# Graph network on one core: three buffers of counts in place of four in the first pass, the fourth's room given to one-hots that are made further ahead, and 53 dense tiles in place of 54

## The chip, the core and the metric

One core of a Trainium2 chip (trn2) runs the whole program. The metric is the device time of one execution in microseconds; it is compared by the median of several runs. The clock of the multiply engine, TensorE (PE in the rows), is granted at one of two levels, 1.2 or 2.4 GHz; a row shows it as a share of the full one.

## What is computed

12500 nodes with 64 features, 212500 directed edges sorted by destination, two layers:

```python
x = x + layer0(relu(layernorm(x)), edge_attr, src, dst)
x = x + layer1(relu(layernorm(x)), src, dst)

def layer0(h, e, src, dst):
    agg = segment_sum(h[src] + e, dst)
    h = relu(agg @ W1 + b1) @ W2 + b2
    return batch_norm(h)

def conv(h, W, b):                       # layer1: conv, relu, conv, relu, then a norm over the graph
    return segment_sum((h @ W)[src] * enorm[:, None], dst) + b
```

So there are three sums over the edges, one for each of three passes, and before each a table of node features is ready in memory.

## The kernel before

**Two ways to sum over edges.** For the first D windows of 125 destination nodes (D = 54 in the first pass, 69 in the other two) the sum is *dense*: a tile of counts A, 12500 sources by 125 destinations in fp8, is multiplied with the table that lies in SBUF (`app`, 100 matmuls for a tile in 25 steps of 4). All other edges are *gathered*: groups of 1280 edges, whose table rows POOL fetches by ten indirect DMAs into one of four slots (`pool_pass`), are summed on PE through a matrix S of destinations (`grp`). The edges' own features, in the first pass alone, are summed in groups too: 167 groups in all, each with an S, a split of the features into three bf16 parts on DVE (`rest1`, `rest2`) and ten matmuls; the groups with a gather have ten more. How many groups have a gather follows from D: `QG` is 88 for 54 tiles, so 79 groups of the first pass are gathered.

**The counts are built on the chip.** A tile of counts comes from 32 products on PE (`bld`) of two one-hots that DVE makes: `oh` (L954, one for a product) and `ob` (L951, one for four products). Each two products fill one of two PSUM banks (`NBANK = 2`), which ACT moves to the tile in SBUF (`evict`, L1204); a product of a new pair waits for the one-hot and for the eviction of the pair two before it:

```python
pe.wait_ge(v_oh, v + 1)
pair, s = v // 2, v % 2
if s == 0 and pair >= NBANK:
    pe.wait_ge(a_ev, pair - NBANK + 1)
```

A finished tile is used by 100 matmuls, and stored to memory (`keep`, 1.6 MB) for the later passes, which load it (`fetch`). The first pass builds all its 54 tiles, the second builds 17 and loads 52, the third loads all 69. Four slots (`NA = 4`) hold tiles of counts. A one-hot lies in one of 6 buffers (`NOH`), an `ob` in one of 3 (`NOB`); DVE waits with a new one until the product that read the buffer is done.

**The order of the work** is written by `make_plan`: every step of an engine gets a due time in units, where one unit is one step of 4 `app` matmuls, and each engine runs its steps in the order of these times, one after another. In the first pass tile q is built from unit 25q, 32 products in 25 units; it is applied from unit 31 + 25q. A group stands every 8 units or so: at t its matmuls, at t + 2.4 the fold of its PSUM on DVE (`fold_q`, L987), at t + 4.6 a transpose on PE (`turn`, L1185; L1189 for a tile's window), 2.1 units later DVE's addition to the accumulator (`add`, L1015, L1020). The next transpose waits for that addition. When all windows of four node blocks are done, a small perceptron runs (`hid`, L1137; `up`, L1140; `hout`, `hmean`, `hvar` on ACT). Due times are no waits: what holds an engine are its semaphores, and the steps queued behind a waiting one.

## Time and profile before

| | |
|---|---|
| median of 3 runs | 4469.84 us (4464.91 to 4476.29) |
| the profiled execution, own time | 4486.21 us |
| its span | 4484.9 us (1.3 us less than its own time) |
| mean granted TensorE clock | 0.809 |
| first pass, first to last fold of a tile (L997) | 219.1 to 1879.9 us |
| busy share of the span | PE 67%, DVE 43%, POOL 42%, ACT 18% |

A busy PE is not PE at its peak, since matmuls overlap: their durations are longer than their distance. The chain of work in the profile names the engine whose work ended last at each step; "remote" and "another core or an unknown queue" stand where the record of a semaphore's rise is missing.

### The profile page before, as it was taken

What the parts mean: (1) busy time and instruction counts of PE and PEld (TensorE: products, weight loads), DVE (VectorE), ACT (ScalarE), POOL (GpSimd) and SP (SyncE); (2) the same over time, 40 slices, a digit from 0 to 9 for tenths busy, and PEclk for the clock granted to TensorE, in tenths of its full rate; (3) what the DMA queues carried; (4) which work ended last, traced back from release to release, by engine and by line L of the source; (5) the groups of instructions that cost most, each with busy time, mean ns of one, the idle gap of its engine ahead of it and who ended that gap; (6) DMA issues with size and microseconds to landing.
All of it is one profiled execution on the core that took longest, in us unless ns stands there. A gap on an engine that the chain in (4) does not pass through costs nothing.

```text
span 4484.9 us, 66591 instructions
## 1 busy us (share of the span) xinstructions
PE 3012.4 (67%) x26545; PEld 2766.3 (62%) x26545; DVE 1926.5 (43%) x4856; ACT 796.3 (18%) x1708; POOL 1861.6 (42%) x1895
## 2 busy tenths in 40 slices
PE   1366676676666667737777777777847777776777
PEld 1365565566556556636666676666846666666667
DVE  9476676767667667742333332323301111111112
ACT  6122222222222223332111111111100000000000
POOL 4554444545444442032444433444134444444441
PEclk9988788878877788858778878888968778878878
DMA  5243333434334333443333333333443333333334
GB/s 125 78 115 100 96 111 99 118 96 116 99 94 114 96 111 101 118 124 119 113 99 114 127 99 127 100 116 126 140 120 113 126 111 127 113 111 119 119 126 123
DMA packets 359879, 504.29 MB, mean 112 GB/s; under 512 B 302486, under 2 KB 302679, under 8 KB 334736
## 3 DMA queue, kind: packets, MB, share of 16 engines
q1 hardware_dynamic: 298437, 402.60, 27.6%
q0 software_dynamic: 60512, 94.12, 9.3%
q8 instruction: 219, 3.59, 0.3%
q10 hardware_dynamic: 616, 3.20, 0.3%
q14 instruction: 95, 0.78, 0.1%
HBM read 362.65 MB, written 137.13 MB: 111 GB/s over the span
## 4 chain that ended last, share of the span: by engine, by line
PE 50%; another core or an unknown queue 17%; issue 14%; DVE 13%; ACT 3%; DVEq 1%; DMA 1%; SPq 0%; POOL 0%; ACTq 0%; POOLq 0%
PE psum L1102 34%; PE psum L1084 6%; DVE arena L954 4%; PE psum L1124 3%; PE psum L1117 3%; DVE arena L980 2%; DVE arena L951 2%; ACT arena L1204 1%; DVEq L1013 1%; PE psum L1067 1%; DVE arena L964 1%; PE psum L1189 1%; PE psum L1137 1%; PE psum L1185 1%
## 5 line engine op out<-in xcount | busy, mean ns | idle before, releaser
L1265 POOL DMA_INDIRECT arena<-table,srcT x1840 | 1800.2, 978 | 2300.3 <-PE psum L1124 1638.2
L1102 PE MATMUL psum<-arena 125*125 125x193 bf16 (+1 forms) x19200 | 2374.5, 274 | 404.9 <-issue 356.6
L1102 PEld LDWEIGHTS psum<-arena 125*125 125x125 fp8e4 x19200 | 2108.8, 157 | 499.6 <-issue 460.6
L1084 PE MATMUL psum<-arena 128*125 128x200 f16 x2272 | 609.0, 287 | 594.4 <-issue 263.0
L954 DVE TENSOR_SCALAR arena<-iota,keyT,oddT 128x200 f16<-128x200 f16 x2272 | 700.8, 336 | 613.2 <-remote 374.4
L1204 ACT CAST arena<-psum 125x400 uint16<-125x400 f32 x1136 | 549.4, 492 | 2148.3 <-PE psum L1084 1236.2
L1084 PEld LDWEIGHTS psum<-arena 128*125 128x125 f16 x2272 | 344.5, 157 | 686.5 <-DVE arena L954 359.4
L951 DVE TENSOR_TENSOR arena<-modT,psum 128x500 f16<-128x500 f16 x568 | 376.4, 663 | 0.1
L964 DVE SCALAR_TENSOR_TENSOR arena<-relT,psum 128x960 bf16<-128x960 f16 x272 | 310.8, 1143 | 0.0
L997 DVE TENSOR_REDUCE arena<-psum 125x64 f32<-125x192 f32 x192 | 67.2, 350 | 562.5 <-PE psum L1102 288.8
L980 DVE TENSOR_TENSOR arena<-arena 128x650 f32<-128x650 f32 (+1 forms) x334 | 274.4, 822 | 7.0 <-DMA arena<-in_edge_attr_dram 4.8
L1117 PE MATMUL psum<-arena 128*96 128x195 bf16 (+1 forms) x1662 | 215.0, 285 | 2.3 <-DVE arena L980 2.3
L1247 ACT ACTIVATE cneg<-cst 125x1 f32<-125x1 f32 x25 | 5.1, 203 | 1189.8 <-DVE arena L1039 1039.0
L987 DVE TENSOR_REDUCE arena<-psum 96x65 f32<-96x195 f32 (+1 forms) x275 | 96.5, 351 | 273.2 <-PE psum L1124 270.9
L1124 PE MATMUL psum<-arena 128*96 128x192 bf16 x1846 | 198.6, 258 | 3.9 <-DMA arena<-table,srcT 3.9
L1117 PEld LDWEIGHTS psum<-arena 128*96 128x96 bf16 (+1 forms) x1662 | 191.1, 145 | 2.8 <-issue 2.5
L1189 PE MATMUL psum<-ident,arena 125*64 125x125 f32 x192 | 60.5, 315 | 190.3 <-DVE arena L997 117.6
L1124 PEld LDWEIGHTS psum<-arena 128*96 128x96 bf16 x1846 | 177.3, 132 | 4.4 <-DMA arena<-table,srcT 4.2
L996 DVE COPY cnt<-psum 125x1 f32<-125x1 f32 x123 | 19.4, 158 | 371.9 <-remote 217.5
L1020 DVE SCALAR_TENSOR_TENSOR acc<-psum,acc 64x125 f32<-64x125 f32 x192 | 53.3, 277 | 270.0 <-remote 192.4
L1015 DVE SCALAR_TENSOR_TENSOR acc<-psum,acc 65x96 f32 (+1 forms) x275 | 68.6, 249 | 205.3 <-PE psum L1185 146.2
L1189 PEld LDWEIGHTS psum<-ident,arena 125*64 125x64 f32 x192 | 23.5, 122 | 215.2 <-issue 188.5
(207 smaller groups left out, 1000.2 us busy)
## 6 DMA issues: line engine op xcount, KB each, us to landing
arena<-counts SPq DMA_DIRECT2D x121, 1600.0 KB
counts<-arena SPq DMA_DIRECT2D x71, 1600.0 KB
arena<-in_edge_attr_dram SPq DMA_DIRECT2D x166, 320.0 KB
arena<-table,srcT POOLq DMA_INDIRECT x1840
table<-arena SPq DMA_DIRECT2D x8, 1050.0 KB
table<-arena SPq DMA_DIRECT2D x25, 168.0 KB
arena<-table SPq DMA_DIRECT2D x4, 1050.0 KB
arena<-in_x_dram ACTq DMA_DIRECT2D x4, 700.0 KB
```

Source lines behind the costliest of these rows:

```text
L951: dve.tensor_tensor(ob(four % NOB), mod, it, ALU.is_equal)
L954: dve.tensor_scalar(oh(v % NOH), iota1[:, :], keyT[:, v:v + 1], oddT[:, v:v + 1], ALU.is_equal, ALU.mult).then_inc(v_oh, 1)
L964: dve.scalar_tensor_tensor(out=S, in0=rel, scalar=0.0, in1=it, op0=ALU.add, op1=ALU.is_equal).then_inc(v_S, 1)
L980: dve.tensor_tensor(ebuf(e, i + 1)[0:parts, 0:nt * FE], a, upper, ALU.subtract).then_inc(v_rest1 if i == 0 else v_rest2, 1)
L987: dve.tensor_reduce(qbuf(n % 2)[:, 0:fe], ps_q.rearrange("p (s f) -> p f s", s=3)[:, 0:fe, :], X, ALU.add).then_inc(v_fq, 1)
L1084: pe.matmul(to, ob(v // NB4 % NOB)[:, v % NB4, :], oh(v % NOH).rearrange("p (j m) -> p j m", m=2), start=True, stop=True).then_inc(p_bld, 1)
L1102: last = pe.matmul(ps_v[n % 2][0:PN, 0:xc], A(slot)[0:PN, j, 0:PN], Xs[0:PN, j, 0:xc], start=(j == 0), stop=(j == J - 1))
L1117: last = pe.matmul(ps_q, S[0:parts, t, :], e3(v % NEDGE)[0:parts, t, :, :], start=(t == 0), stop=(t == nt - 1 and not gathered))
L1124: last = pe.matmul(to, S[0:parts, t, :], gbuf(slot)[0:parts, t, :].rearrange("p (s f) -> p s f", s=3), start=(k > 0 and t == 0), stop=(t = ...
L1189: pe.transpose(ps_g[0:F, 0:PN], vbuf(m % 2)[0:PN, :], ident[0:PN, 0:PN]).then_inc(p_win, 1)
L1204: act.copy(A2(slot)[0:PN, :, i // 2 * SUB:(i // 2 + 1) * SUB], ps_b[b // 2 % NBANK][0:PN, :].rearrange("p (j x) -> p j x", x=SUB)).then_in ...
L1265: pool.indirect_dma_start(out=gbuf(slot)[0:parts, t, :], out_offset=None, in_=tables[k], in_offset=bass.IndirectOffsetOnAxis(ap=idx, axis= ...
```

## The change

In the first pass alone, tiles of counts use three slots (`NA0 = 3`) and not four. The room of the fourth holds 14 more `oh` and 4 more `ob`, so that 20 and 7 are there in place of 6 and 3. DVE makes a product's one-hot 14 units ahead of it, where it was 3.3 (14 units are 18 products, 3.3 units are 4). S, `rest1` and `rest2` of a group are put 3 units earlier, the load of its edges 2 units earlier. `hmean` and `hvar` are put about a unit later. The first pass has 53 dense tiles, which the three slots ask for (`D0 % NA0 == 2`), so `QG` is 87 and 80 groups are gathered; the second pass builds 18 tiles, one in three from the seventh on, and loads 51. The x load at the end of the first pass goes where slots 2 and 3 are, so it waits for all products too.

```diff
-NOH = 6
+NOH = (20, 6)
-NOB = 3
+NOB = (7, 3)
 NA = 4
+NA0 = 3
-DENSE = (54, 69, 69)
+DENSE = (53, 69, 69)
...
-            if n_b < len(built) and q >= 6 and (q - 5) * len(built) >= n_b * (D - 7):
+            if n_b < len(built) and q >= 6 + 3 * n_b:
...
-                dve.append((t - 3.3, "oh", b))
+                dve.append((t - (14.0 if k == 0 else 3.3), "oh", b))
...
-        dve.append((t - 7.0, "S", n))
+        dve.append((t - (10.0 if k == 0 else 7.0), "S", n))
         if k == 0:
-            sp.append((t - 12.5, "edges", n))
-            dve.append((t - 5.2, "rest1", n))
-            dve.append((t - 4.2, "rest2", n))
+            sp.append((t - 14.5, "edges", n))
+            dve.append((t - 8.2, "rest1", n))
+            dve.append((t - 7.2, "rest2", n))
...
-            act.append((t + 6.2, "hmean", i))
-            act.append((t + 6.4, "hvar", i))
+            act.append((t + 7.3, "hmean", i))
+            act.append((t + 7.4, "hvar", i))
...
+        def slot_of(k, q):
+            return q % NA0 if k == 0 else (plans[k]["s0"] + q) % NA
...
-                    if v >= NOH:
-                        dve.wait_ge(p_bld, v - NOH + 1)
+                    if v >= noh:
+                        dve.wait_ge(p_bld, v - noh + 1)
...
-                        if q >= NA:
-                            act.wait_ge(p_app, n - NA + 1)
+                        if q >= (NA0 if k == 0 else NA):
+                            act.wait_ge(p_app, n - (NA0 if k == 0 else NA) + 1)
...
                 sp.wait_ge(p_app, D0 - 2)
-                for i in (2, 3):
-                    sp.wait_ge(st_cnt[i], kept[0][i])
+                sp.wait_ge(p_bld, NB0)
+                sp.wait_ge(st_cnt[2], kept[0][2])
```

What this does to DVE's order shows at two places. The first is DVE at the start of the first pass (L951 and L954 are `ob` and `oh` of before, L964 is S, L980 a `rest`); before:

```order
L951 TENSOR_TENSOR arena<-modT,psum 128x500
L954 TENSOR_SCALAR arena<-iota,keyT,oddT 128x200 x4
L951 TENSOR_TENSOR arena<-modT,psum 128x500
L954 TENSOR_SCALAR arena<-iota,keyT,oddT 128x200 x3
L964 SCALAR_TENSOR_TENSOR arena<-relT,psum 128x960
```

and of the changed kernel, where the same steps have the lines L965, L968 and L978:

```order
L965 TENSOR_TENSOR arena<-modT,psum 128x500
L968 TENSOR_SCALAR arena<-iota,keyT,oddT 128x200 x4
L965 TENSOR_TENSOR arena<-modT,psum 128x500
L968 TENSOR_SCALAR arena<-iota,keyT,oddT 128x200 x4
L965 TENSOR_TENSOR arena<-modT,psum 128x500
L968 TENSOR_SCALAR arena<-iota,keyT,oddT 128x200 x4
L965 TENSOR_TENSOR arena<-modT,psum 128x500
L968 TENSOR_SCALAR arena<-iota,keyT,oddT 128x200 x4
L965 TENSOR_TENSOR arena<-modT,psum 128x500
L968 TENSOR_SCALAR arena<-iota,keyT,oddT 128x200
L978 SCALAR_TENSOR_TENSOR arena<-relT,psum 128x960
```

Ahead of the first S there stand 17 one-hots of products where there were 7.

The second place is DVE in the middle of the first pass, from one group's `add` on (L1015; L987 is `fold_q`); before:

```order
L1015 SCALAR_TENSOR_TENSOR acc<-psum,acc 65x96
L954 TENSOR_SCALAR arena<-iota,keyT,oddT 128x200
L951 TENSOR_TENSOR arena<-modT,psum 128x500
L954 TENSOR_SCALAR arena<-iota,keyT,oddT 128x200 x2
L964 SCALAR_TENSOR_TENSOR arena<-relT,psum 128x960
L954 TENSOR_SCALAR arena<-iota,keyT,oddT 128x200 x2
L987 TENSOR_REDUCE arena<-psum 96x65
L951 TENSOR_TENSOR arena<-modT,psum 128x500
L954 TENSOR_SCALAR arena<-iota,keyT,oddT 128x200
L980 TENSOR_TENSOR arena<-arena 128x650
L954 TENSOR_SCALAR arena<-iota,keyT,oddT 128x200
L980 TENSOR_TENSOR arena<-arena 128x650
```

and of the changed kernel (L1029 is the `add`, L994 a `rest`, L1001 the `fold_q`, L978 S):

```order
L1029 SCALAR_TENSOR_TENSOR acc<-psum,acc 65x96
L968 TENSOR_SCALAR arena<-iota,keyT,oddT 128x200 x2
L994 TENSOR_TENSOR arena<-arena 128x650
L968 TENSOR_SCALAR arena<-iota,keyT,oddT 128x200
L994 TENSOR_TENSOR arena<-arena 128x650
L965 TENSOR_TENSOR arena<-modT,psum 128x500
L968 TENSOR_SCALAR arena<-iota,keyT,oddT 128x200 x2
L1001 TENSOR_REDUCE arena<-psum 96x65
L968 TENSOR_SCALAR arena<-iota,keyT,oddT 128x200 x2
L965 TENSOR_TENSOR arena<-modT,psum 128x500
L968 TENSOR_SCALAR arena<-iota,keyT,oddT 128x200 x3
L978 SCALAR_TENSOR_TENSOR arena<-relT,psum 128x960
```

Before, S stands ahead of the fold and the two `rest` behind it; in the changed kernel the two `rest` stand ahead of the fold and S behind it.

## Rows read from the trace of the kernel before

**Rows 1.** The page: span, busy time of each engine, granted clock by slice.

```profile
span 4484.9 us, 66591 instructions
PE 3012.4 (67%) x26545; PEld 2766.3 (62%) x26545; DVE 1926.5 (43%) x4856; ACT 796.3 (18%) x1708; POOL 1861.6 (42%) x1895
```

**Rows 2.** Windows: window, length, busy of five engines (count), clock, DMA.

```profile
200.00:1740.00 1540.00, 1026.24 (x8633) 926.87 (x8630) 1076.19 (x2739) 403.86 (x867) 739.11 (x720) 0.81 0.38 104
1740.00:1880.00 140.00, 114.58 (x1064) 101.62 (x1064) 122.15 (x316) 49.11 (x108) 2.25 (x2) 0.92 0.44 131
2050.00:3200.00 1150.00, 839.89 (x7515) 783.30 (x7513) 367.65 (x1073) 156.68 (x335) 466.27 (x492) 0.81 0.35 112
```

**Rows 3.** One line, L997 (a tile's fold), 200 to 1740, then 1740 to 1885.

```profile
L997 DVE TENSOR_REDUCE arena<-psum x47: 337/344/358, 219.1 to 1719.2; 125x64 f32<-125x192 f32 x47
L997 DVE TENSOR_REDUCE arena<-psum x7: 339/344/347, 1752.9 to 1879.9; 125x64 f32<-125x192 f32 x7
```

**Rows 4.** Windows of 4 us over one burst of gathers.

```profile
840.00:844.00 4.00, 2.60 (x28) 2.27 (x27) 4.00 (x12) 1.15 (x3) 3.09 (x4) 1.00 0.46 102
844.00:848.00 4.00, 2.23 (x24) 1.88 (x21) 0.46 (x3) 0.49 (x1) 3.09 (x4) 1.00 0.20 44
848.00:852.00 4.00, 0.00 (x0) 0.00 (x0) 1.33 (x2) 0.00 (x0) 2.34 (x3) 0.88 0.21 42
852.00:856.00 4.00, 2.34 (x15) 2.37 (x16) 2.97 (x7) 1.38 (x3) 0.00 (x0) 0.50 0.36 82
```

**Rows 5.** Timeline, 846 to 854: start, length, engine, what, [idle before it].

```profile
846.42 0.36 PE L1084 MATMUL psum<-arena 128*125 128x200 f16 x2 [0.89 <-issue]
...
853.02 0.89 ACT L1204 CAST arena<-psum 125x400 uint16<-125x400 f32 x2 [6.75 <-remote]
853.03 0.33 DVE L954 TENSOR_SCALAR arena<-iota,keyT,oddT 128x200 f16<-128x200 f16 x1 [3.69 <-remote]
...
853.63 0.18 PEld L1084 LDWEIGHTS psum<-arena 128*125 128x125 f16 x1 [6.70 <-DVE arena L954]
853.66 0.40 PE L1084 MATMUL psum<-arena 128*125 128x200 f16 x1 [6.54 <-ACT arena L1204]
```

**Rows 6.** Waits, 200 to 1850: total us, times, longest.

```profile
PEld psum L1084 <- DVE arena L954: 291.9, 146, 8.0
DVE arena L954 <- remote: 259.8, 112, 6.7
...
PE psum L1084 <- ACT arena L1204: 199.6, 78, 7.8
...
DVE arena L954 <- PE psum L1084: 171.2, 175, 3.2
...
PEld psum L1137 <- DVE acc L1015: 24.5, 17, 3.6
PEld psum L1189 <- DVE acc L1015: 22.2, 16, 2.6
...
PEld psum L1185 <- DVE acc L1020: 13.9, 13, 3.0
...
DVE arena L980 <- DMA arena<-in_edge_attr_dram: 2.4, 2, 1.4
```

**Rows 7.** Timeline: first and last product that waited for a one-hot.

```profile
241.07 0.35 PEld L1084 LDWEIGHTS psum<-arena 128*125 128x125 f16 x2 [0.76 <-DVE arena L954]
...
1837.88 0.13 PEld L1084 LDWEIGHTS psum<-arena 128*125 128x125 f16 x1 [0.54 <-DVE arena L954]
```

**Rows 8.** Lines by form, 200 to 1850: gathers on POOL.

```profile
L1265 POOL DMA_INDIRECT arena<-table,srcT x720 | 739.3, 1027 | 802.5 <-PE psum L1124 601.8 <-issue 197.5 <-remote 3.1
```

**Rows 9.** Timeline, 1346 to 1355: a store of counts, then loads of edges.

```profile
1346.06 0.33 SPq L1303 DMA_DIRECT2D counts<-arena  x1
...
1346.43 5.74 SPq L1299 DMA_DIRECT2D arena<-in_edge_attr_dram  x2
...
1354.27 0.84 DVE L980 TENSOR_TENSOR arena<-arena 128x650 f32<-128x650 f32 x1 [1.04 <-DMA arena<-in_edge_attr_dram]
```

More of the change, by code:

```diff
@@ L210, in bass_gnn_preln_kernel @@
     SHIFT = RED * NSUB
-    assert NSUB % NB4 == 0 and NB4 * PN % 2 == 0 and 2 * KC <= 512 and NROW * P <= E and NC * P <= 5 * 512 and D0 % NA == 2 and NSUB % 2 == 0
+    assert NSUB % NB4 == 0 and NB4 * PN % 2 == 0 and 2 * KC <= 512 and NROW * P <= E and NC * P <= 5 * 512 and D0 % NA0 == 2 and NSUB % 2 == 0
     assert NBLD - SEED <= 2048 and SUB == 4 and P % NSUB == 0
@@ L234, in bass_gnn_preln_kernel @@
         n_oh = KC // 2
-        o_ob = o_oh + NOH * n_oh
+        o_ob = o_oh + NOH[1] * n_oh
         n_ob = NB4 * PN // 2
-        o_hb = o_ob + NOB * n_ob
+        o_hb = o_ob + NOB[1] * n_ob
+        o_ox = o_A + NA0 * n_A
+        n_ox = (NOH[0] - NOH[1]) * n_oh + (NOB[0] - NOB[1]) * n_ob
+        assert n_ox < (NA - NA0) * n_A
         o_g = max(o_hb + 2 * JH * PN, o_e + JF)
@@ L329, in oh @@
         def oh(k):
-            return part(o_oh, k, n_oh).bitcast(F16)
+            at = part(o_oh, k, n_oh) if k < NOH[1] else part(o_ox, k - NOH[1], n_oh)
+            return at.bitcast(F16)
         def ob(k):
-            return part(o_ob, k, n_ob).bitcast(F16).rearrange("p (n d) -> p n d", d=PN)
+            o = o_ox + (NOH[0] - NOH[1]) * n_oh
+            at = part(o_ob, k, n_ob) if k < NOB[1] else part(o, k - NOB[1], n_ob)
+            return at.bitcast(F16).rearrange("p (n d) -> p n d", d=PN)
         def ebuf(k, i=0):
@@ L526, in sp_load @@
                              a.rearrange("(a b) -> a b", a=1).broadcast_to([P, 1])).then_inc(l_w, 16)
-            n = NA * n_A
-            spare = x.rearrange("p n -> (p n)")[0:(P - PN) * n].rearrange("(a n) -> a n", n=n)
-            sp.dma_start(arena[PN:P, o_A:o_A + n], spare).then_inc(l_spare, 16)
+            for a, b in ((o_A, o_ox), (o_ox + n_ox, o_w)):
+                spare = x.rearrange("p n -> (p n)")[0:(P - PN) * (b - a)].rearrange("(a n) -> a n", n=b - a)
+                sp.dma_start(arena[PN:P, a:b], spare).then_inc(l_spare, 16)
         LN_ORDER = (3, 2, 0, 1)
@@ L901, in bass_gnn_preln_kernel @@
             for q, (kind, w) in enumerate(pl["seq"]):
-                slot = (pl["s0"] + q) % NA
+                slot = slot_of(k, q)
                 kept_before[k, q] = n_kept[slot]
@@ L1083, in pe_pass @@
                     to = ps_b[pair % NBANK][0:PN, :].rearrange("p (j s m) -> p j s m", s=2, m=2)[:, :, s, :]
-                    pe.matmul(to, ob(v // NB4 % NOB)[:, v % NB4, :], oh(v % NOH).rearrange("p (j m) -> p j m", m=2), start=True,
+                    pe.matmul(to, ob(v // NB4 % NOB[k])[:, v % NB4, :],
+                              oh(v % NOH[k]).rearrange("p (j m) -> p j m", m=2), start=True,
                               stop=True).then_inc(p_bld, 1)
@@ L1088, in pe_pass @@
                     n = pl["d0"] + q
-                    slot = (pl["s0"] + q) % NA
+                    slot = slot_of(k, q)
                     if i == 0:
@@ L1196, in act_pass @@
                     n = pl["d0"] + q
-                    slot = (pl["s0"] + q) % NA
+                    slot = slot_of(k, q)
                     if i == 1:
-                        if q >= NA:
-                            act.wait_ge(p_app, n - NA + 1)
+                        if q >= (NA0 if k == 0 else NA):
+                            act.wait_ge(p_app, n - (NA0 if k == 0 else NA) + 1)
                         if kept_before[k, q]:
@@ L1284, in sp_fetch @@
             pl = plans[k]
-            slot = (pl["s0"] + v) % NA
+            slot = slot_of(k, v)
             if kept_before[k, v]:
@@ L1300, in sp_pass @@
                 elif kind == "keep":
-                    slot = (pl["s0"] + v) % NA
+                    slot = slot_of(k, v)
                     sp.wait_ge(a_ev, last_b[k, v])
@@ L1799, in sp_first @@
             sp.wait_ge(v_set, 1)
-            sp.wait_ge(l_spare, 16)
+            sp.wait_ge(l_spare, 2 * 16)
         def pe_second():
```

11 lines of the change are left out of this document (7 added, 4 removed).

## The prediction

> **What bounds the kernel now.** The page comes first: the span is 4484.9 us and no engine fills it, PE comes nearest with 67% [rows 1]. So the limit is in how the engines wait for each other, and it has to be read by stage. The windows cut the run into stretches [rows 2]. In the first pass, while gathers run (200 to 1740), PE is busy 67% and DVE 70% (1076 of 1540 us). In its last 140 us, when the gathers are over, PE is busy 82% and DVE 87%. In the second pass DVE has 32%. The folds of the tiles give the pace [rows 3]: with gathers (1719.2 - 219.1) / 46 = 32.6 us for a tile, without them (1879.9 - 1752.9) / 6 = 21.2 us. The gathers are what makes a tile long, though POOL itself often waits for PE, 601.8 us of 1650 [rows 8].
>
> Windows of 4 us over one burst of ten gathers show how [rows 4]. At its start DVE is full (4.00 of 4.00). From 844 on PE fades, from 848 to 852 it does nothing and DVE a third. Then it starts again at clock 0.50. The timeline says what ends this [rows 5]: the two products that PE issued at 846.42 are seen by ACT and by DVE only at 853.02 and 853.03, when the burst is over, and PE goes on at 853.63. So semaphores that PE raises during a burst reach the others late, by up to some 6 us, and PE stops when it meets a wait whose answer depends on one of them.
>
> **Which wait that is** decides what this change can do. The waits view names both [rows 6]: the load of a product's weights (PEld) is put down to DVE's one-hot with 291.9 us, the multiplication (PE) to ACT's eviction with 199.6 us. It is the same idle time under two names, as in rows 5 (6.70 and 6.54 us). To part them I took each of the 1654 products between 200 and 1850 and compared the start of its load with the end of its own one-hot and of the eviction that it needs. 219 products stand behind more than 0.3 us of idle, 475.6 us in all. In 194 of them, 461.3 us, the eviction ended last; in 25, 14.4 us, the one-hot did; the first and the last of these 25 stand in [rows 7]. PE is stopped by the two PSUM banks, and the change leaves them at two.
>
> **The change part by part.**
>
> *The moved tile.* The first pass loses 100 `app` matmuls and 32 products. Without gathers 140 us hold 1064 matmuls, 0.132 us each [rows 2]: -17.4 us. By the stretch with gathers (1540 / 8633 = 0.178 us) it would be -23.5; I take the first, since a burst's stop belongs to the burst.
>
> *One more gathered group.* Bursts per tile: 72 groups (720 gathers) in 1540 / 32.6 = 47.2 tiles, 1.53 [rows 2, 3, 8]. One costs (32.6 - 21.2) / 1.53 = 7.5 us. Lower bound: the idle of one stop, some 5 us; upper: a burst's whole length, 10 x (1.03 + 0.30) = 13.3 us [rows 8]. I take +7.5.
>
> *32 products more in the second pass*, at 1150 / 7515 = 0.153 us a matmul [rows 2]: +4.9 us. A store takes the place of a load; DMA engines are at 0.35 there, so that costs nothing. The new spacing of the built tiles only shifts work.
>
> *One-hots ahead.* Freed of every wait for a one-hot, PE gains at most the 14.4 us. DVE gains no lead: with 20 buffers and 18 products ahead it waits for the product that is two before PE's place, and so it did with 6 and 4. So its own waits in front of L954, 259.8 + 171.2 us [rows 6], stay, and during a stop DVE is held nearly as before. What PE gains is that DVE may fall behind by 14 units where 3.3 were allowed. But a group's transpose stands only 2.2 units behind its fold, and PE waits already for additions and folds before L1137, L1189 and L1185, 24.5 + 22.2 + 13.9 = 60.6 us [rows 6]. Some of the gain is paid there. I take -8 us, bounds 0 and -14.
>
> *Order on DVE.* The two `rest` (0.83 us each) now stand before the fold and S (1.14 us) behind it, so the fold comes about 0.5 us of work later, against 2.2 units, 1.9 to 2.9 us at these paces. The edges' load is 2 units earlier, its reader 3 units. In the rows DVE waited for edges 2.4 us in all [rows 6]. A load that is queued behind a store of counts lands 8 us after its issue [rows 9]. Measured for all 167 groups, 16 have less than 4 us between landing and use; 3 units are 3.9 us at 32.6 us a tile. If each used up its slack, DVE would wait 41 us more, mostly under the one-hots that it has ahead. I take +3 us on PE.
>
> *Three slots.* Tile q is last read at unit 56 + 25q, the tile q + 3 first written at 76 + 25q: 20 units, 17 to 26 us by rows 3. The store has 50 units, 42 us or more, and needs under 8 by rows 9. No wait; without this cover each tile would pay what is missing. *The x load* now waits for the last product, about 32 units before the last tile ends, some 27 us; at the pace of rows 9 (1.6 MB of counts and 0.3 MB of edges within 8 us) its 3.1 MB take some 13 us. *The start*: ten more one-hots before the first S are done while PE waits for the first gathers. *hmean, hvar*: the same work on an ACT that is a quarter busy. I cost these three at nothing, with 5 us of doubt on the load.
>
> The sum: -17.4 + 7.5 + 4.9 - 8 + 3 = **-10 us**. The profiled execution took 4486.2 us, so it becomes 4476. The median of the runs is 16.4 us lower, at 4469.84, so I predict **4460 us**.
>
> **The rivals.**
>
> A, the forecast: the stops stay, PE's gain is small. 0.50.
>
> B, *the deep buffers do pay*. DVE is full at the start of a burst and a third busy in the stop [rows 4]; if PE can run ahead of it, DVE works its debt off in the stop. Then the 14.4 us go and the 60.6 us of the transposes with them, -75 us, net of the tile -80: 4390. If half of it comes, 4425. For it speaks that DVE outside the stops has hardly any idle time left: 1076 / 47.2 = 22.8 us of work in a tile of 32.6, of which 1.53 stops of some 5 us take 8. Against it: the lead is the same, and the transposes bind at 2.2 units. 0.22.
> The same rows show that PE comes back at 0.50 of the clock after a stop and had 1.00 before [rows 4]. The Trainium skill, "TensorE: Matmul & The Clock Gate", section "HAM oscillation — how this bites in real kernels", says that idle gaps between stretches of matmuls put the clock back to half, each time anew. By that rule a shortened stop would give a second gain in the work behind it, so B would be larger than its waits; where the stops stay, as in A, it gives nothing. The trace agrees on the fall.
>
> C, *slower: the edges and the earlier `rest` hold DVE*. The mechanism is DVE standing at a `rest` whose edges have not landed, with the fold and the addition queued behind it, for which PE's transpose waits. It decides once DVE is more than 2.2 units behind. If all 41 us reach PE in place of the 3, the sum is +28: 4498; with the 27 us that 3 us of shift give, +14: 4484. 0.18.
>
> D, *the order does nothing that can be seen* and only the tile's move counts, -5 us, with the bursts falling elsewhere against the waits, 10 us either way: 4465. 0.10.
>
> **How the numbers follow.** The likeliest is A, 4460, its own range 4445 to 4475. The range of 4420 to 4490 takes in the better part of B and C and leaves out some 2 in 10. What a measurement of this kernel can tell from no change is about 0.3%, 13.4 us. Faster by more: all of B and 0.18 of A, with 0.02 of D, 0.42. Slower by more: C but for 0.03, with 0.02 of A and 0.03 of D, 0.20. The rest, 0.38, is the same.
>
> **What the profile after would show.** The wait of PEld L1098 (the products) for one-hots nearly unchanged as named, the eviction still last in most; a stop of the same length in each burst; DVE's idle time before L968 still some 400 us; the fold's pace still near 32.5 us with gathers, and 53 of them, not 54, in the first pass. B is right if the pace falls below 31 us and DVE is busier than 70%. C shows as waits of DVE at L994 for edges, tens of us, and longer ones of PE at L1200 and L1204. An eviction that waits for a slot, or a longer gap between the passes, would mean that the cover of three slots or of the x load was misread. I would be wrong altogether if PE's late semaphores depended on what DVE does in a burst.

## The result, and the profile after

The changed kernel took 4487.3 us, median of 20 runs (4459.4 to 4511.2), beside 4469.93 us for 20 runs of the kernel before on the same chip. The ratio is 1.0039 with a 95% interval of 1.0020 to 1.0057. So the change made the kernel slower, by 17 us. That lies inside the forecast range of 4420 to 4490, but it is a loss where the likeliest value, 4460, was a gain of 10.

The profiled execution took 4479.34 us, less than its median, as that of before took more than its own (4486.2 against 4469.8). The two profiles therefore differ by -7 us where the medians differ by +17. They can show what moved, and not a difference of this size; the experiments below have to.

First the page of the changed kernel: span, and busy time of each engine.

```profile
span 4477.7 us, 66410 instructions
PE 2999.6 (67%) x26454; PEld 2760.1 (62%) x26454; DVE 1924.9 (43%) x4853; ACT 792.5 (18%) x1708; POOL 1871.3 (42%) x1905
```

The windows of the first pass with gathers, of its end, and of the second pass, as in [rows 2]:

```profile
200.00:1740.00 1540.00, 1020.17 (x8593) 927.47 (x8591) 1075.75 (x2728) 399.00 (x861) 739.17 (x722) 0.79 0.37 105
1740.00:1870.00 130.00, 106.75 (x964) 95.12 (x964) 103.68 (x261) 43.50 (x97) 9.11 (x10) 0.88 0.44 126
2050.00:3200.00 1150.00, 838.83 (x7505) 783.72 (x7504) 374.35 (x1103) 162.65 (x350) 463.42 (x490) 0.80 0.35 114
```

The folds of the tiles (one line, L1011, before L997), as in [rows 3]:

```profile
L1011 DVE TENSOR_REDUCE arena<-psum x47: 335/346/350, 217.0 to 1736.1; 125x64 f32<-125x192 f32 x47
L1011 DVE TENSOR_REDUCE arena<-psum x6: 336/342/349, 1767.7 to 1870.9; 125x64 f32<-125x192 f32 x6
```

The waits, 200 to 1850, as in [rows 6]. L1098 is a product, L968 a one-hot, L1219 an eviction, L1152, L1200 and L1204 are PE's transposes, L994 a `rest`.

```profile
POOL arena L1280 <- PE psum L1139: 612.1, 72, 11.4
ACT arena L1219 <- remote: 530.5, 134, 8.1
PEld psum L1098 <- DVE arena L968: 278.6, 119, 7.9
DVE arena L968 <- remote: 266.1, 141, 5.3
...
PE psum L1098 <- ACT arena L1219: 188.6, 71, 7.7
DVE arena L968 <- PE psum L1098: 163.4, 164, 3.7
...
PEld psum L1152 <- DVE acc L1029: 16.7, 11, 3.0
PEld psum L1204 <- DVE acc L1029: 16.7, 13, 2.6
...
PEld psum L1200 <- DVE acc L1034: 11.0, 11, 2.6
...
DVE arena L994 <- DMA arena<-in_edge_attr_dram: 7.2, 5, 2.6
```

Almost nothing in these waits tells a faster kernel from a slower one. DVE's own wait at the one-hots is 429.5 us, against 431.0 in [rows 6]. A tile with gathers takes (1736.1 - 217.0) / 46 = 33.0 us against 32.6 in [rows 3]: 19 us over 47 tiles, about what the shorter pass had saved. Waits for the edges grew from 2.4 to 7.2 us only. The pass lengths say where to look. The last `app` of the first pass starts at 1870.5 us (1879.5 before), the second pass lasts 1289.6 us (1287.4), the third 1200.5 (1201.5). What happens, happens in the first pass.

There I cut the trace by the bursts of gathers; gathers less than 1.5 us apart count as one burst. For each burst I summed the time in which PE does nothing (gaps over 0.3 us) from the burst's start to 3 us past its end. Before it is 6.92 us for ten gathers, after it is 7.12, and the first stop of over 2 us begins on the mean 8.05 us behind the burst's start before and 6.77 us after. PE stops earlier, and in both it goes on, on the mean, about 1 us after the burst's end. This measure is used below for the variants.

### The profile page after: what moved, and what is told of

Its sections match the earlier page's. It is cut to its first block, busy times and chain, and to the rows that moved or that the text cites. A ratio compares the mean times of both kernels' runs of the same rounds, so it can differ in the third digit from the quotient of the medians.

```text
span 4477.7 us, 66410 instructions
## 1 busy us (share of the span) xinstructions
PE 2999.6 (67%) x26454; PEld 2760.1 (62%) x26454; DVE 1924.9 (43%) x4853; ACT 792.5 (18%) x1708; POOL 1871.3 (42%) x1905
## 4 chain that ended last, share of the span: by engine, by line
PE 52%; another core or an unknown queue 19%; issue 13%; DVE 10%; ACT 3%; DVEq 1%; DMA 1%; SPq 0%; POOL 0%; ACTq 0%; POOLq 0%
PE psum L1117 35%; PE psum L1098 6%; PE psum L1139 3%; DVE arena L968 3%; PE psum L1132 2%; ACT arena L1219 2%; DVE arena L965 1%; PE psum L1081 1%; DVEq L1027 1%; DVE arena L994 1%; DVE arena L978 1%; PE psum L1200 1%; PE psum L1152 1%; PE psum L1204 1%
## 5 line engine op out<-in xcount | busy, mean ns | idle before, releaser
L1098 PE MATMUL psum<-arena 128*125 128x200 f16 x2272 | 615.3, 289 | 616.5 <-issue 306.7
L968 DVE TENSOR_SCALAR arena<-iota,keyT,oddT 128x200 f16<-128x200 f16 x2272 | 697.3, 334 | 581.3 <-remote 365.6
L1219 ACT CAST arena<-psum 125x400 uint16<-125x400 f32 x1136 | 549.2, 492 | 2126.0 <-PE psum L1098 1114.7
L1098 PEld LDWEIGHTS psum<-arena 128*125 128x125 f16 x2272 | 350.1, 160 | 711.2 <-issue 386.9
L965 DVE TENSOR_TENSOR arena<-modT,psum 128x500 f16<-128x500 f16 x568 | 375.9, 662 | 0.2
L978 DVE SCALAR_TENSOR_TENSOR arena<-relT,psum 128x960 bf16<-128x960 f16 x272 | 310.4, 1141 | 0.0
L1011 DVE TENSOR_REDUCE arena<-psum 125x64 f32<-125x192 f32 x191 | 66.8, 350 | 565.7 <-PE psum L1117 287.0
L994 DVE TENSOR_TENSOR arena<-arena 128x650 f32<-128x650 f32 x334 | 274.5, 822 | 11.9 <-DMA arena<-in_edge_attr_dram 11.1
L1001 DVE TENSOR_REDUCE arena<-psum 96x65 f32<-96x195 f32 (+1 forms) x275 | 96.4, 351 | 285.5 <-PE psum L1139 282.4
L1132 PE MATMUL psum<-arena 128*96 128x195 bf16 x1662 | 206.1, 277 | 3.8 <-DVE arena L994 3.8
L1132 PEld LDWEIGHTS psum<-arena 128*96 128x96 bf16 x1662 | 182.0, 139 | 4.7 <-issue 4.2
L1204 PE MATMUL psum<-ident,arena 125*64 125x125 f32 x191 | 60.4, 316 | 181.9 <-DVE arena L1011 120.3
L1139 PEld LDWEIGHTS psum<-arena 128*96 128x96 bf16 x1856 | 171.7, 129 | 1.0 <-DMA arena<-table,srcT 0.7
L1029 DVE SCALAR_TENSOR_TENSOR acc<-psum,acc 65x96 f32 (+1 forms) x275 | 68.4, 249 | 208.7 <-PE psum L1200 151.4
L1204 PEld LDWEIGHTS psum<-ident,arena 125*64 125x64 f32 x191 | 23.4, 123 | 202.6 <-issue 179.6
```

The costliest lines, as they stand in the source:

```text
L965: dve.tensor_tensor(ob(four % nob), mod, it, ALU.is_equal)
L968: dve.tensor_scalar(oh(v % noh), iota1[:, :], keyT[:, v:v + 1], oddT[:, v:v + 1], ALU.is_equal, ALU.mult).then_inc(v_oh, 1)
L978: dve.scalar_tensor_tensor(out=S, in0=rel, scalar=0.0, in1=it, op0=ALU.add, op1=ALU.is_equal).then_inc(v_S, 1)
L994: dve.tensor_tensor(ebuf(e, i + 1)[0:parts, 0:nt * FE], a, upper, ALU.subtract).then_inc(v_rest1 if i == 0 else v_rest2, 1)
L1001: dve.tensor_reduce(qbuf(n % 2)[:, 0:fe], ps_q.rearrange("p (s f) -> p f s", s=3)[:, 0:fe, :], X, ALU.add).then_inc(v_fq, 1)
L1098: pe.matmul(to, ob(v // NB4 % NOB[k])[:, v % NB4, :], oh(v % NOH[k]).rearrange("p (j m) -> p j m", m=2), start=True, stop=True).then_inc(p ...
```

## The experiments: the change taken apart

All of these run on one core; the ratio is always to runs of the kernel before **on the same chip at the same time**, since the chips turned out to differ. The first four were run on one chip, where before took 4456.07 us.

**The tile alone.** The changed kernel with every other edit undone, but for three slots and the new order of built tiles:

```
-NOH = (20, 6)          +NOH = (6, 6)
-NOB = (7, 3)           +NOB = (3, 3)
 one-hots 14.0 -> 3.3, S 10.0 -> 7.0, edges 14.5 -> 12.5,
 rests 8.2/7.2 -> 5.2/4.2, hmean/hvar 7.3/7.4 -> 6.2/6.4
```

> 53 dense tiles, three slots of counts and the new spacing of built tiles, with the one-hots, their 6 and 3 buffers and all due times of DVE, SP and ACT as before. Theory M (the moved tile costs: one burst of gathers more in the first pass and 32 products more in the second outweigh the matmuls saved): slower than before by 10 us or more, about as the whole change (ratio 1.003 to 1.004). Rival O (the loss comes from the order on DVE, not from the tile): within 8 us of before or faster, by the sum of the prediction -5 us.

Measured 4447.84 us, ratio 0.9978 (0.9956 to 1.0001): -8 us. The sum of the prediction's three terms for it was -5. This part holds, and all of what follows is against this kernel.

**One-hots 14 ahead with 20 and 7 buffers**, the group steps where they were:

```
 e1_tile with
+NOH = (20, 6)
+NOB = (7, 3)
+dve.append((t - (14.0 if k == 0 else 3.3), "oh", b))
```

> The kernel of the label before (53 tiles, three slots) with 20 and 7 one-hot buffers and the one-hots made 14 units ahead; groups' steps on DVE as before. Theory P (PE may now run ahead of DVE's one-hots, but its two PSUM banks stop it just as before): the same as with the tile alone, within 8 us. Rival O: 10 to 20 us slower than with the tile alone, since one-hots that are made 14 units early keep more urgent work of DVE (folds, additions) waiting.

Measured 4485.84 us, ratio 1.0070 (1.0044 to 1.0096): +38 us against the tile alone. The forecast had -8.

**The same buffers, one-hots left at 3.3 ahead:**

```
 e1_tile with
+NOH = (20, 6)
+NOB = (7, 3)
```

> As the label before, with 20 and 7 buffers, but the one-hots due 3.3 units ahead as in the kernel before, so that DVE's wait for a free buffer is 16 products behind and hardly ever holds it. If DVE's lead is what was missing (the prediction said that 20 buffers with 18 products ahead give no lead): DVE's idle time in front of its one-hots falls from some 430 us to under 150, and the time falls by 10 to 40 us against the tile alone. If the two PSUM banks hold PE whatever DVE does: that idle time moves to DVE's other lines and the time stays within 8 us.

Measured 4402.64 us, ratio 0.9883 (0.9847 to 0.9918): -45 us against the tile alone, and faster than the kernel before (by the ratios, than the changed kernel too). One number in the order, 14.0 or 3.3, makes 83 us. Here is what it does: with 20 buffers and a place 18 products ahead DVE stands at the one-hot until a product two before PE's place is done. With 20 buffers and the old place it has a reach of 16 products in which it never stands. "Place" is the due time in the order; "reach" is how many products further than its place a free buffer would let DVE go. The waits of this kernel, 200 to 1850:

```profile
DVE arena L1001 <- remote: 154.9, 45, 8.3
PEld psum L1098 <- DVE arena L968: 139.3, 91, 7.3
PE psum L1098 <- DVE arena L968: 72.3, 42, 7.0
DVE acc L1029 <- remote: 65.4, 18, 9.9
```

DVE L968, first of DVE's rows before and after, has no wait left at all. What remains stands at the group's fold (L1001) and at the additions. The wait of PE's weight loads that is named after the one-hots is 139.3 us, where it is 298.9 with the tile alone. The stops cost PE less: 473 us in all by the measure above, against 506 in the kernel with the tile alone. Part of that is visible as a change of form. In ten places a second group's gathers follow the first's without a pause, one burst of twenty, and such a burst cost PE 10.6 us, where two single ones cost 2 x 6.8.

**The group steps alone:** S, the `rest`s and the edges 2 to 3 units earlier, buffers and one-hots as before:

```
 e1_tile with
+dve.append((t - (10.0 if k == 0 else 7.0), "S", n))
+sp.append((t - 14.5, "edges", n))
+dve.append((t - 8.2, "rest1", n))
+dve.append((t - 7.2, "rest2", n))
```

> 53 tiles and three slots with the one-hots as before, but S, both rests and the edges' loads of a group earlier as in the change. Rival C of the prediction (DVE stands at a rest whose edges have not landed, and the fold behind it is late): 10 us or more slower than with the tile alone, waits of DVE for edges over 20 us. Otherwise within 8 us of the tile alone.

Measured 4493.48 us, ratio 1.0074 (1.0047 to 1.0100): +46 us against the tile alone. The forecast had +3, and +41 only if DVE waited for edges. It does not. What changes is what DVE does around a burst's start. Windows of 4 us over one burst each, which starts at 1041.96 with the tile alone and at 873.01 here (columns as in [rows 2]). Of the tile alone, all work, and then the line of the `rest`s (L994; only DVE's busy time):

```profile
1038.00:1042.00 4.00, 4.00 (x28) 4.00 (x26) 1.59 (x3) 0.00 (x0) 0.04 (x1) 0.52 0.00 0
1042.00:1046.00 4.00, 3.70 (x34) 2.71 (x32) 3.71 (x10) 2.29 (x5) 3.08 (x4) 1.00 0.44 107
1046.00:1050.00 4.00, 2.58 (x27) 2.22 (x25) 1.36 (x4) 1.71 (x6) 3.09 (x4) 1.00 0.22 48
1050.00:1054.00 4.00, 0.00 (x0) 0.00 (x0) 0.38 (x1) 0.00 (x0) 3.09 (x4) 0.76 0.18 42
...
1038.00:1042.00 4.00, 0.00 (x0) 0.52 0.00 0
1042.00:1046.00 4.00, 1.65 (x2) 1.00 0.44 107
```

And with the group steps earlier:

```profile
869.00:873.00 4.00, 4.00 (x41) 4.00 (x40) 4.00 (x10) 1.12 (x3) 0.00 (x0) 0.83 0.00 0
873.00:877.00 4.00, 3.48 (x40) 3.32 (x39) 4.00 (x12) 1.83 (x4) 3.07 (x4) 1.00 0.49 113
877.00:881.00 4.00, 1.53 (x18) 1.34 (x15) 2.09 (x6) 0.00 (x0) 3.15 (x3) 0.95 0.18 37
881.00:885.00 4.00, 1.21 (x6) 0.94 (x6) 1.32 (x3) 0.49 (x1) 3.33 (x3) 0.50 0.60 229
...
869.00:873.00 4.00, 1.65 (x2) 0.83 0.00 0
873.00:877.00 4.00, 0.00 (x0) 1.00 0.49 113
```

The group's two `rest`s (1.65 us) stand in the burst's first 4 us in the one and ahead of the burst in the other, and PE works 2.58 us of the second 4 us in the one, 1.53 in the other. That is one burst of each. Over all bursts of ten between 200 and 1740, the first stop of over 2 us begins 7.79 us after the start with the tile alone, 7.62 with one-hots 14 ahead, 6.59 with the group steps earlier and 6.77 in the changed kernel. PE's idle time in all bursts of the pass is 506, 532, 546 and 522 us. Against 506, that is +26, +40 and +16 us, where the medians of the first two differ by +38 and +46 us (the changed kernel itself was not timed beside them). So most of either loss is in the stops of the bursts. The two shifts do not seem to be additive: moved together, as the change does, PE's idle time grew by less than with either alone.

The traces show one thing more, for each eviction at which ACT had been idle: how long after the end of the second product of its pair it began. For products that end 2 to 4 us behind a burst's start this is 1.15 us in the median with the tile alone and 2.79 with the group steps earlier; from 4 to 6 us, 2.44 and 5.89. So the semaphores that PE raises in a burst are themselves seen later when the group steps stand earlier, though the order of PE's and ACT's steps is unchanged. With one-hots 14 ahead it is 1.45 and 2.85, close to the tile alone.

## The experiments: why PE stops

The prediction said that PE is stopped by the two PSUM banks. These three ran on a second chip, where before took 4361.02 us. A matmul's semaphore that is seen late, as in [rows 5], is called a late semaphore from here on. The third bank needs room, so the iota that DVE reads in each small one-hot and each S moves from PSUM bank 2 to SBUF; a control does only that. The last one is the changed kernel with both.

```
 before, control             bank                        changed kernel, bank
+iotah = sb("iotah", [P, P], F16)   +NBANK = 3           both, in the changed kernel
-ps_i = psum[:, 2, 0:P]             +ps_b in banks (0, 1, 2)
+ps_i = iotah[:, 0:P]
```

> The kernel before with the row of numbers that DVE compares with (iota) in SBUF as fp16 and not in PSUM bank 2: the control of the next label. DVE's one-hots for four products and its S may get faster or slower by their operand; expected within 1% of before.

> As the control, with bank 2, now free, as a third PSUM bank for products. Theory: PE is stopped in a burst because the evictions of two pairs are all it may run ahead of, so a third bank lets it do two products and their share of other work more, some 1.3 us, in each of the 140 or so bursts of the first two passes: 60 to 150 us faster than the control. Rival: PE would be stopped by something else right behind (fold, addition), less than 20 us.

> The changed kernel with iota in SBUF and the third PSUM bank. If the banks were what kept the deep one-hots from paying: faster than the third bank on the kernel before, by 10 us or more. If not: the same or slower than that, by the 17 us that the change costs.

Measured 4099.74 us, ratio 0.9397 (0.9356 to 0.9439) for the control, 4093.96 us, 0.9389 (0.9355 to 0.9423) with the third bank, and 4129.16 us, 0.9469 (0.9423 to 0.9515) for the changed kernel with both. The bank adds nothing that can be measured to the control. PE's waits at a product for the eviction, 200 to 1850, first in the control, then with the third bank:

```profile
PE psum L1085 <- ACT arena L1205: 50.6, 34, 8.4
...
PE psum L1085 <- ACT arena L1205: 23.8, 17, 6.0
```

They were 199.6 us in [rows 6], so the control had already taken most of them away, and the bank was never tried where the eviction ended nearly all of the stops. Against the banks in the kernel before speaks rather `e3_deep_late`: it has two of them as well, and its deep buffers gained 45 us. An eviction that ends last can do so because its own input, PE's semaphore, is late, without being short of room. The change still costs 35 us in a kernel with the moved iota and three banks. And the control, meant to do nothing, is 6% faster, in all three passes and ahead of them: its first `app` starts at 142.1 us, where it is 183.8 in the profile before. Its row of gathers, 200 to 1560, beside [rows 8]:

```profile
L1266 POOL DMA_INDIRECT arena<-table,srcT x719 | 988.5, 1375 | 318.2 <-issue 213.4 <-PE psum L1125 93.9 <-remote 10.9
```

A gather takes 1375 ns in place of 1027, and POOL waits 93.9 us for PE where it waited 601.8. PE's semaphores are less late: of 566 evictions behind a product that ends in a burst, 2 us or more from its start, ACT begins 0.04 us after the product in the median and 1.91 in the ninth tenth, where the kernel before has 2.45 and 7.41. Now both operands of S and of the small one-hots lie in SBUF. The Trainium skill, "SBUF — State Buffer", section "🔬 SBUF: two separate sides", says that a DVE operation with two SBUF inputs and a GpSimd operation that reads SBUF share one pair of ports, as a lock. The longer gathers agree with it (a gather reads its row numbers, `srcT`, from SBUF), and by that rule alone the control could be slower or the same, not faster. Two theories for the gain were left: gathers that come less densely leave PE's semaphores less late (the spacing theory), or DVE's reads of PSUM were in the way (the PSUM theory).

## The experiments: on chips where nothing is late

The next four were to part these theories, and the group shift from the one-hots. For the group shift there were two accounts: the spacing theory (without the `rest`s in its way a burst's gathers follow each other faster, and PE's stop begins earlier) and the queue theory (what is lost is DVE standing at one-hots with the group's work behind it, so that the shift costs nothing once DVE never stands there). In these four runs before took 2998.67 us. This was another chip, and the same program is a third shorter on it.

```
 e10_deep_groups: the changed kernel, one-hots at 3.3 again
 e11_pace: before, and in the first pass ahead of each gather but a group's first, twice
+    pool.iota(scr[:, :], pattern=[[1, 96]], base=0, channel_multiplier=0)
 e13_sbuf_ob, e12_sbuf_S: before, with only the small one-hots, or only S, reading the iota in SBUF
```

> The changed kernel (tile, 20 and 7 buffers, group steps earlier), with the one-hots of the first pass again due 3.3 units ahead. Against e3_deep_late only the group steps' places differ. Spacing theory: an operation of DVE with two SBUF operands holds back POOL's gathers; with the two rests ahead of a burst and not in its first 3 us, the first gathers follow each other faster and PE's stop begins earlier (onset 8.05 us after the burst's start before, 6.59 in e4_groups); deep room does not help, so it costs some 0.6 us in each of 78 bursts, about 45 us: 0.998 of the kernel before. Queue theory: what e4_groups lost came from DVE standing at one-hots with the groups' work queued behind; with room for 20 it does not stand, so the groups' shift costs nothing: 0.988, as e3_deep_late.

> The kernel before, and ahead of each gather but the first of a group in the first pass POOL writes two small iotas (96 numbers each, one after the other) into a scratch tensor that nobody reads: the gathers of a burst come about 0.6 us further apart, nothing else is changed, DVE's iota still in PSUM. Spacing theory: PE's semaphores come late because of how densely gathers follow; the stops shrink as in e6_iota, ratio 0.96 to 0.985 (the first pass alone is paced; in e6_iota it was 240 of the 375 us). Rival, PSUM theory (e6_iota won because DVE no longer read PSUM): gathers that come later only delay the groups and stretch each burst by 6 us, ratio 1.00 to 1.03.

> The kernel before; only the small one-hots (ob, one for four products, 0.66 us) read their iota from SBUF, S still from PSUM. e6_iota moved both: 0.940. Spacing theory: each such operation in a burst holds POOL once; ob stands for 2.0 us of a burst and S for 1.2, so ob carries some five eighths: 0.96. PSUM theory: by elements read, 8 x 500 a tile against 1.5 x 960, three quarters: 0.955. If one of the two carries all, it is its place in the burst that counts, not how much is read.

> The kernel before; only S (one for each group, 1.14 us) reads its iota from SBUF, the small one-hots still from PSUM. Spacing theory: three eighths of what e6_iota gained, 0.975. PSUM theory: a quarter, 0.985. Passes 1 and 2 have more groups for each product, so S should carry most of what is gained there.

Measured 0.9765 (0.9743 to 0.9787), 1.0364 (1.0339 to 1.0388), 1.0053 (1.0037 to 1.0068) and 1.0131 (1.0109 to 1.0153). None of these could decide what it was for. What they do show is that the moved iota, 6% faster on the second chip, is a loss here for each of its two readers. The next runs, on a fourth chip of the same kind (before 2995.47 us), are the paced kernel once more, the changed kernel itself, the same with one-hots at 3.3, and the deep buffers together with the moved iota.

> The changed kernel itself, unedited. The chips differ: before took 4356 to 4488 us on three and 2998.67 us on the one of the last call, where PE's end is seen by ACT after 0.04 us at all times, while on the others it takes up to 7 us within a burst. On a chip with late semaphores (before above 4300): 1.004 as on record. On a chip without: late-semaphore theory says that the loss hangs on the stops, so without them the change gives what its tile and its 14 units of lead are worth, 0.975 to 0.985, near the 0.9765 of e10_deep_groups. Rival: one-hots placed 14 ahead make DVE stand before its group work at any time; then it loses to e10_deep_groups by over 1% there too.

> e10_deep_groups again, beside f1_after on one chip: they differ in one number, 14.0 against 3.3 for the one-hots. On a chip with late semaphores, spacing theory 0.998, queue theory 0.988 (as put on record for e10_deep_groups, which ran on a chip that could not decide it). On a chip without: 0.976.

> e11_pace again (two small iotas of POOL between the gathers of the first pass). On a chip with late semaphores, spacing theory 0.96 to 0.985, PSUM theory 1.00 to 1.03. On a chip without, 1.036 as measured: there the pace of the gathers bounds, and what is added to each is paid.

```
 e9_deep_sbuf: e3_deep_late with
-ps_i = psum[:, 2, 0:P]
+ps_i = iotah[:, 0:P]
```

> e3_deep_late (tile, 20 and 7 buffers, one-hots 3.3 ahead, group steps as before) with the iota in SBUF as e6_iota. On a chip with late semaphores e6_iota gave 0.940 and e3_deep_late 0.988; if they are two causes the product is 0.929; if the deep room only bridged the stops that the iota in SBUF removes, 0.938. On a chip without late semaphores the iota in SBUF costs (e12_sbuf_S 1.013, e13_sbuf_ob 1.005, together 1.018) and the deep room gives 0.976: 0.994.

The changed kernel took 2956.31 us, ratio **0.9872** (0.9852 to 0.9891): on this chip the change is a gain of 39 us. With one-hots at 3.3, 2933.17 us, 0.9791 (0.9773 to 0.9809). Paced, 3114.17 us, 1.0398 (1.0371 to 1.0424). Deep with the moved iota, 3223.41 us, 1.0752 (1.0730 to 1.0773), where I expected 0.994: a loss with the moved iota here too.

The page and the windows of the changed kernel on this chip: the first pass, and 400 us of the second.

```profile
span 2948.9 us, 66410 instructions
...
200.00:1300.00 1100.00, 885.24 (x8597) 814.39 (x8596) 1047.53 (x2736) 407.09 (x873) 789.72 (x724) 0.93 0.53 147
1700.00:2100.00 400.00, 396.51 (x4542) 393.08 (x4541) 234.55 (x697) 106.76 (x227) 291.84 (x307) 1.00 0.60 201
```

DVE is busy 95% of the first pass, PE 99% in the second, at the full clock. A product's end and the eviction that waits for it, in the timeline of this run:

```profile
701.35 0.25 PE L1098 MATMUL psum<-arena 128*125 128x200 f16 x1
...
701.64 0.49 ACT L1219 CAST arena<-psum 125x400 uint16<-125x400 f32 x1 [0.37 <-PE psum L1098]
```

The product ends at 701.60, in the middle of a burst, and ACT begins at 701.64. I took this difference for each eviction at which ACT had been idle (200 to 1300), from the end of the second product of its pair. On this chip it is 0.04 us in the median and in the ninth tenth of all 588, and 0.11 at most. In the profile of before (200 to 1740) it is 0.04 in the median and 0.11 at most outside the bursts; inside, from 2 us on, it is 2.45 in the median, 7.41 at the ninth tenth and 9.25 at most. The waits view tells it more simply: in the profile after, ACT and DVE wait 530.5 and 266.1 us for "remote"; in this run no row names "remote". PE's stops go with the late semaphores, and so do the second and third pass at 1290 and 1200 us in place of 749 and 713; that these lengths come from the late semaphores alone is not shown. The Trainium skill, "TensorE: Matmul & The Clock Gate", section "HAM oscillation — how this bites in real kernels", has idle gaps put the clock back; where most of the gaps are gone the granted clock is 0.93 in place of 0.80 in the same 1100 us, which agrees.

Even so the place of the one-hots counts here: 14.0 in place of 3.3 costs 2956.31 - 2933.17 = 23 us. The waits from 200 to 1300 show where. The changed kernel:

```profile
PE psum L1200 <- DVE arena L1001: 94.7, 69, 2.5
PEld psum L1200 <- DVE acc L1034: 62.0, 27, 4.3
POOL arena L1280 <- PE psum L1139: 60.7, 28, 5.9
...
DVE arena L968 <- PE psum L1098: 46.2, 47, 3.5
```

With the one-hots at 3.3:

```profile
PEld psum L1098 <- DVE arena L968: 85.4, 143, 1.7
...
PE psum L1200 <- DVE arena L1001: 51.5, 68, 1.9
...
PEld psum L1200 <- DVE acc L1034: 38.4, 27, 2.5
```

DVE stands 46.2 us at one-hots whose buffer is not free, with the group's fold (L1001) and the additions queued behind; with the old place it never does. PE's transpose waits for the fold 94.7 us in place of 51.5. That is the price of the lead in the order: PE no longer waits for one-hots (under 20 us in place of 85.4) and waits longer for folds.

The last result on this chip, the deep buffers with the moved iota, in its row of gathers from 200 to 1300:

```profile
L1281 POOL DMA_INDIRECT arena<-table,srcT x612 | 915.6, 1496 | 186.6 <-issue 186.6
```

POOL waits for nobody any more, only its issue time is left between the gathers: with 1496 ns for a gather it has become the bound. Perhaps the deep room, which lets DVE work through the bursts, makes it worse; that is not shown. Two costs that I had multiplied (1.018 and 0.976) do not multiply.

**The group shift again, on a chip with late semaphores** (a fifth one; before 4354.06 us), with deep buffers and one-hots at 3.3 in both. The edits are those of `e3_deep_late` and `e10_deep_groups`.

> e3_deep_late again (tile, 20 and 7 buffers, one-hots due 3.3 ahead, group steps as before), beside g2 on one chip. Late semaphores (before above 4300): 0.988 as measured. Without (before near 3000): queue theory says that the group steps' place does not matter once DVE never stands at a one-hot, 0.978 like g2; spacing theory says the same, for there is no stop to start earlier.

> g1 with the group steps earlier, as in the changed kernel. Without late semaphores 0.978 (measured 0.9765 and 0.9791). With late semaphores: spacing theory, the rests leave the burst's first 3 us and PE's stop begins earlier, 0.998; queue theory, no difference to g1, 0.988.

Measured 4287.91 us, 0.9861 (0.9789 to 0.9933), and 4358.15 us, 0.9988 (0.9951 to 1.0025). So the group shift costs 70 us, some 35 either way by the two intervals, also where DVE never stands at a one-hot, and the queue theory falls for it. (In this pair `hmean` and `hvar` are later too. In the two profiles the first pass is 49 us longer.) The spacing theory had said 0.998. PE's idle time from 4 to 8 us after a burst's start is 100 us in all in place of 67, and the semaphores are later as in the first pair: 2.02 us in the median in place of 0.04 for products that end 2 to 4 us behind the start. But the theory's account of the size does not hold in full. With the `rest`s in a burst's first 3 us, its fourth gather starts at 4.32 us, without them at 3.82 (4.31 and 3.86 in the pair on the first chip). That is the half microsecond by which the gathers are held, and it is little more than a third of the 1.2 us by which the stop came earlier in the first pair. In this pair the first long stop hardly moved (7.83 and 7.68 us). What differs besides is that with the old group steps 13 bursts have the gathers of two groups or more, against 7 with the new ones, and that the idle time in all bursts is 412 us against 453.

**Pacing, a third time:**

> The kernel before, with two small iotas of POOL between the gathers of the first pass, as f3_pace. If the chip has late semaphores (before above 4300): spacing theory, PE's stops shrink though DVE still reads PSUM, pass 0 becomes shorter by 50 us or more, ratio 0.96 to 0.985; PSUM theory, 1.00 to 1.03. If it has none, 1.04 once more.

Measured 3111.81 us, 1.0399 (1.0370 to 1.0427), on a chip without late semaphores again (before 2993.8 us). There the group's first matmul waits for the gathers (118.9 us from 200 to 1300, against 1.8 with one-hots at 3.3 on the chip before), and the pace is paid. Whether spacing or PSUM made the control of the second chip faster stays open.

## Why the prediction was wrong

- **The tile** (-17.4 + 7.5 + 4.9 = -5 us): -8 us. Right, within the interval of 10 us either way. That the later passes do not change was right as well.
- **Order on DVE** (+3 us): the step that failed. Alone it measured +46 us, and +70 us beside the deep buffers. It was priced by how late the fold and the edges come, and neither moved: waits for edges 7.2 us, the waits of PE at L1152, L1200 and L1204 44.4 us, where they had been 60.6. What I did not price is what DVE has left to do while a burst runs. The rows for it stood there: [rows 4] show DVE full in the burst's first 4 us and a third busy in the stop. The runs showed in its place that these steps, put earlier, make PE's semaphores later in the burst (1.15 to 2.79 us) and its stops come 1.2 us earlier.
- **One-hots ahead** (-8 us): the second step that failed. The lead in products is the same, as I said, and DVE's wait at the one-hots stayed at 430 us, as I said. But the conclusion, a small gain, was wrong. Together with its buffers the shift cost 38 us; the buffers alone gained 45. On a chip without late semaphores one can see the shift's price by itself, 23 us, paid at the fold. There 14 units of one-hots stand ahead of each group's steps.
- **"PE is stopped by the two PSUM banks"**: wrong as a bound. With two banks kept, deep buffers gained 45 us, and a third bank beside the moved iota gave nothing; beside the iota in PSUM it was not run. That the eviction ended last in 461.3 of 475.6 us was read rightly from the trace, and showed the order in which late semaphores are answered. So deep buffers could pay although PE hardly ever waited for a one-hot by that count.
- **Three slots, x load, start, `hmean`**: at nothing, and no row speaks against it: the gap between the first two passes is 83.5 us against 81.7. `hmean` and `hvar` were not tried alone.
- **Rival B** (deep buffers pay) was right that they can, and it was refused for the right reason: it needs a real lead, and the change gives none. With the lead it is -45 us for the buffers, not -75, and not where B put the larger part: PE's weight loads wait 48.1 us at L1152, L1200 and L1204 with the lead and 49.9 with the tile alone. **Rival C** came nearest in time, 4484 against 4487.3, by a mechanism that did not happen. **Rival D** holds for the later passes only.
- The last sentence of the prediction named what would make it wrong altogether: that PE's late semaphores depend on what DVE does in a burst. They do, and the stops with them. The four variants on one chip differ only in DVE's and SP's order and in the buffers, and by 91 us (4402.64 to 4493.48).

The parts do not add up on one chip, for none ran all of them. By ratios: deep buffers with the group shift and one-hots at 3.3 are 0.9988 on the fifth chip, or -5 us; the one-hots' place costs 23 us where it was measured beside it, on a chip without late semaphores. Together +18 us, against +17 measured. This mixes chips of both kinds and is an estimate.

What is shown: which edits cost and gain, and that most of it is in the bursts of the first pass, where PE's semaphores are later with the group steps earlier. What is not: by what the group steps' place delays a semaphore, beyond the half microsecond of the held gathers, and why deep buffers with one-hots 14 ahead cost 38 us where semaphores are late. The version to keep is 20 and 7 buffers with the one-hots at 3.3 and the old group steps: 0.9883 and 0.9861 of before on two chips with late semaphores. With the new group steps it is 0.9765 and 0.9791 where none is late, but only 0.9988 where they are. The old group steps were run on a chip of the second kind only beside the moved iota.

## What to carry to other kernels

In this kernel more buffers helped only while the producer's place in its queue stayed late: move it ahead by as much as the room grew and it stands as often as before, now with more work of others behind it. When an eviction or a semaphore ends an idle time, ask whether its own input was late before calling it the bound; add the missing resource beside a control that has the same side edits, and look whether the control still has the wait that the resource is to end. And time such a change on more than one chip: this one is +0.4% on one kind and -1.3% on the other, and a planner's numbers tuned on one need not suit the other.

## What the runs showed of the hardware

- Of the chips used, one kind takes 4338 to 4488 us for the kernel before (four sets of runs, the first comparison among them, and all executions but one), another 2986 to 3006 us (three sets). On the first kind ACT began up to 9.25 us after the end of the product that it waited for while gathers ran, on the second after 0.04 us, at most 0.11. Why is open; nothing in the program differs.
- On the first kind, the order of DVE's and SP's work changes how late PE's semaphores are: 1.15 or 2.79 us in the median for products that end 2 to 4 us behind its start, in two kernels that differ in the place of S, the `rest`s and the edges alone.
- Moving a 128 x 128 iota that DVE reads from PSUM to SBUF (and to fp16) made gathers longer (1027 to 1375 ns) and the kernel 6% faster on the first kind; on the second kind S alone from SBUF cost 1.3% and the small one-hots alone 0.5%, and all of it with deep buffers 7.5%. DVE's own operations did not change (663 and 665 ns for a small one-hot).
- Two iotas of 0.23 us between gathers cost 3.6 to 4.0% where the gathers are near the bound.
